# A vision tower on one core: third bf16 part on GpSimd, the rows of the maxima sent a step sooner, twelve more unread products, five projections moved forward

## The chip, the core and the metric

The kernel runs on one core of a Trainium2 chip. The core has TensorE (PE, matrix products into PSUM), VectorE (DVE), ScalarE (ACT), GpSimd (POOL) and SyncE (SP, which here only issues transfers); they run on their own and wait for each other by semaphores. The metric is the device time of one execution in microseconds. An execution is timed several times, and one more is run with the hardware profiler.

## The reference

The input holds four sequences of 512 tokens of 256 channels. Four blocks follow, each but the first with a residual sum and a layer norm:

```python
h = relu(x @ W0.T) * (x @ W1.T) @ Wo.T                  # gated unit, DE = 512
h = layernorm(h + window_attention(h))                  # 16 heads of 16, |i - j| <= 64
h = layernorm(h + quantised_ffn(h))                     # 8-bit activations, ternary weights, 1024 wide
h = layernorm(h + causal_attention(h))                  # 16 heads of 16
scores = softmax(h @ wg); gates, idx = top_k(scores, 2) # 8 experts, capacity 640 rows each
y = combine(gates, expert(dispatch(h, idx)))            # silu(x @ fc1.T + b1) @ fc2 + b2
out = layernorm(h + y) * gamma + beta
```

Softmax, norms and the expert layers are in float32. The scores of the attention must keep float32 accuracy.

## The kernel before, in words

**Two halves.** Up to about 603 us the kernel computes everything before the experts, then the eight experts one after the other (until about 898 us), then the last norm. The change touches the first part and the seam between the two.

**Half steps.** The first part is a pipeline that is written out by hand. A unit `u` is one tile of 128 keys for four heads of one batch; there are 128 units, 64 of the window attention and 64 of the causal one. Every unit takes two half steps, `eta`, and each engine runs through the same list `HALVES` of half steps and does in each what is due: TensorE the scores of half step `eta` and the transposed scores, values and back transposes of units that began 15, 19 and 28 half steps earlier (`TO_TURNED`, `TO_VALUES`, `TO_BACK`). A batch has 32 half steps, numbered 32 i to 32 i + 31 for the eight pairs (layer, batch) i. In the profile a half step takes some 2 us.

**Dense work.** The table `DENSE` (L98) says at which half step the other phases of each batch begin: `tok` the gated unit, `qkv` the projections, `o` the output projection and its norm, `ffn` the quantised layer, `gate`, `route` and `send` the routing. `STEPS` says how many steps a phase has, and `stretched` (L154) puts the steps of a `qkv` phase from batch 2 on two half steps apart. In each half step an engine does its attention work and then `dense` for each phase in the order of the table. The eight PSUM banks are dealt out by `take` (L179) from the same table, so the banks follow a change of it.

**Projections in three parts.** A float32 projection is kept as three bf16 parts whose products add up to float32 accuracy. Step c of `qkv` has TensorE make piece j = c − 1 (queries and keys of eight heads, two blocks: four pieces), ScalarE copy it twice from PSUM, as float32 into `proj` (L766, two buffers) and as bf16 into `parts` (L767). One step later VectorE takes the difference in place (L1340) and GpSimd rounds it to the second part (L598). One step later still VectorE takes the rest as the third part (L1335). SyncE copies the parts into the stacks `qs` and `ks` (L499), a ring of three blocks of heads, twelve transfers of 128 KB a block; it waits for the ring place, and ScalarE waits with the next batch's piece for the copies of the last (`stack_in`) and for the third part two pieces back (`part2_done`).

**Rows of the maxima.** The transposed scores need the negated row maxima as three more rows of `qs`. VectorE finds the maxima (L1156), GpSimd splits them into three parts (`split_maxima`, L577 to L583), TensorE turns them (L874), ScalarE copies them out (`rows`, L659) in half step 8 g + 11 and issues the transfer into `qs` (`send_rows`, L666) at the start of half step 8 g + 12, after all that it does in step 8 g + 11. TensorE reads them with the transposed scores of step 8 g + 15 (L889).

**Port to the experts.** After the last row transfer of the routing (L619) the rows of expert 0 are loaded and turned (L1547), and the first layer (L1562) follows. To keep TensorE from standing still, 26 products whose result nobody reads (L1582) run before, released by GpSimd seven transfers into the last `send`.

## Time and profile before

| | |
|---|---|
| median of 3 runs | 938.91 us (934.48 to 941.21) |
| profiled execution | 940.09 us, span 938.2 us |
| PE busy | 838.0 us, 89% |
| DVE busy | 513.8 us, 55% |
| ACT busy | 434.0 us, 46% |
| POOL busy | 342.1 us, 36% |
| mean granted clock | 0.947 |
| L1335, third part | 32, 23.4 us of DVE |
| L1340, difference | 32, 24.4 us of DVE |
| L598, second part | 32, 20.8 us of POOL |
| L1582, unread products | 26, 7.3 us of PE |

The span is that of the instructions; the rest of an execution's time lies around it. Busy time is counted per engine over the whole span, so a share of it says nothing of a stretch in which another engine is the one waited for. The granted clock is that of TensorE, 1.0 being 2.4 GHz and 0.5 being 1.2 GHz.

### The profile page before, as it was taken

The page shows a single profiled execution, that of the slowest core. Times are in us where ns is not written, and L with a number is a line of the kernel's source. Part 1 is how long each engine was busy: PE and PEld are TensorE (multiplying, and loading weights), DVE is VectorE, ACT ScalarE, POOL GpSimd, SP SyncE. Part 2 cuts the span into 40 slices and gives each one's busy share as a digit, 9 for nine tenths or more (in the row PEclk, how much of TensorE's full clock was granted, in tenths as well). Part 3 has the DMA queues.
Part 4 walks back from the last instruction along what each step waited for, and adds up shares of the span by engine and source line. Part 5 has one row for each costly group of instructions (what it writes and reads, how often), then busy time and mean ns, then how long its engine had stood idle before and what let it go on. Part 6 is the DMA issues. An engine that isn't in the chain of part 4 may idle for free.

```text
span 938.2 us, 14078 instructions
## 1 busy us (share of the span) xinstructions
PE 838.0 (89%) x4784; PEld 537.0 (57%) x4784; DVE 513.8 (55%) x1929; ACT 434.0 (46%) x794; POOL 342.1 (36%) x517
## 2 busy tenths in 40 slices
PE   6999999898898899899999897499999999999920
PEld 2565546555555455355454354267787787887820
DVE  5676335779798798688887763230220221221246
ACT  1525335687787887887566563122112112112006
POOL 6124224635445343233463634620220320321422
PEclk9999999999999899999898997789999999999965
DMA  9662021212211220210333106311514514512342
GB/s 341 210 233 72 24 69 51 61 29 69 70 34 38 69 65 11 64 52 19 114 92 92 48 24 241 109 51 45 152 18 135 151 17 135 147 22 61 35 111 90
DMA packets 58663, 81.48 MB, mean 87 GB/s; under 512 B 8160, under 2 KB 52193, under 8 KB 56160
## 3 DMA queue, kind: packets, MB, share of 16 engines
q1 hardware_dynamic: 49520, 70.48, 23.4%
q0 software_dynamic: 7296, 9.47, 6.0%
q10 hardware_dynamic: 1776, 0.63, 0.3%
q8 instruction: 38, 0.62, 0.3%
q14 instruction: 33, 0.27, 0.1%
HBM read 35.37 MB, written 19.68 MB: 59 GB/s over the span
## 4 chain that ended last, share of the span: by engine, by line
PE 69%; DVE 15%; issue 5%; ACT 5%; POOL 3%; DMA 2%; SPq 0%; ACTq 0%; POOLq 0%; DVEq 0%
PE ps L1562 15%; PE ps L1576 15%; PE ps L956 6%; PE ps L905 5%; PE ps L1002 4%; DVE junk L1156 4%; PE ps L867 4%; PE ps L889 4%; PE ps L1028 3%; PE ps L973 3%; PE ps L922 2%; PE ps L1011 2%; ACT probs L681 1%; DVE sm L1306 1%; PE ps L932 1%
## 5 line engine op out<-in xcount | busy, mean ns | idle before, releaser
L1156 DVE CUSTOM_DVE_ANT_0 junk<-ps,maskb 128x256 bf16<-128x256 f32 (+4 forms) x512 | 200.3, 435 | 74.1 <-PE ps L867 73.8
L681 ACT ACTIVATE probs<-ps 128x512 f32<-128x512 f32 (+1 forms) x304 | 157.3, 552 | 66.9 <-PE ps L889 64.8
L1600 ACT ACTIVATE hTe<-ps,qs 128x640 f32<-128x640 f32 x64 | 50.8, 794 | 221.1 <-PE ps L1562 221.1
L1517 POOL DMA_INDIRECT mixed_rows<-ysb,ids x40 | 62.0, 1551 | 223.9 <-DVE ysb L1675 220.9
L1576 PE MATMUL ps<-ks,hTe 128*128 128x256 f32 x640 | 143.3, 379 | 0.0
L1562 PE MATMUL ps<-dxT,qs 128*128 128x320 f32 x512 | 142.8, 439 | 0.5 <-DVE dxT L1653 0.5
L1576 PEld LDWEIGHTS ps<-ks,hTe 128*128 128x128 f32 x640 | 119.3, 190 | 15.1
L1562 PEld LDWEIGHTS ps<-dxT,qs 128*128 128x128 f32 x512 | 98.5, 193 | 41.0 <-issue 2.0
L889 PE MATMUL ps<-qs,ks 99*128 99x256 bf16 (+4 forms) x512 | 104.0, 289 | 10.8 <-DMA qs<-nrows 5.6
L867 PE MATMUL ps<-ks,qs 96*128 96x256 bf16 (+4 forms) x512 | 106.0, 290 | 2.9 <-DVE nmax L1156 1.4
L905 PE MATMUL ps<-probs,vaug 128*32 128x256 f32 (+4 forms) x1024 | 89.9, 425 | 7.5 <-POOL probs L557 3.8
L867 PEld LDWEIGHTS ps<-ks,qs 96*128 96x128 bf16 x512 | 44.3, 100 | 81.2 <-issue 64.0
L1653 DVE COPY dxT<-ps 128x256 f32<-128x256 f32 x40 | 16.8, 420 | 130.4 <-PE ps L1547 130.4
L562 POOL TENSOR_SCALAR_AFFINE_SELECT probs<-probs 128x256 f32<-128x256 f32 (+1 forms) x64 | 41.0, 641 | 109.6 <-ACT probs L681 109.6
L1672 DVE TENSOR_TENSOR ysb<-ps,ks 128x256 f32<-128x256 f32 x40 | 17.0, 425 | 110.2 <-PE ps L1576 110.2
L956 PE MATMUL ps<-x_sb,tokw 128*128 128x512 f32 x128 | 62.6, 624 | 7.5 <-DMA tokw<-w 7.5
L557 POOL TENSOR_SCALAR_AFFINE_SELECT probs<-probs 128x512 f32<-128x512 f32 x64 | 41.0, 642 | 73.1 <-ACT probs L681 72.9
L889 PEld LDWEIGHTS ps<-qs,ks 99*128 99x128 bf16 x512 | 43.8, 100 | 37.2 <-DVE nmax L1156 7.8
L1002 PE MATMUL ps<-actT,aw 128*128 128x512 f32 x128 | 60.5, 598 | 1.9 <-issue 1.1
L905 PEld LDWEIGHTS ps<-probs,vaug 128*32 128x32 f32 x1024 | 20.8, 110 | 38.7 <-issue 24.3
L1156 DVE DVE_READ_ACCUMULATOR2_ANT nmax<- 128x1 f32 x512 | 42.3, 83 | 0.0
L956 PEld LDWEIGHTS ps<-x_sb,tokw 128*128 128x128 f32 x128 | 23.6, 198 | 31.8 <-issue 31.6
(198 smaller groups left out, 1223.8 us busy)
## 6 DMA issues: line engine op xcount, KB each, us to landing
qs<-parts SPq DMA_DIRECT2D x96, 128.0 KB, 2.4
ks<-parts SPq DMA_DIRECT2D x96, 128.0 KB, 2.4
qs<-w SPq DMA_DIRECT2D x8, 1024.0 KB, 9.4
ks<-w SPq DMA_DIRECT2D x8, 1024.0 KB, 4.9
dispatched_rows<-att SPq DMA_DIRECT2D x8, 650.0 KB, 10.6
ks<-dispatched_rows SPq DMA_DIRECT2D x4, 650.0 KB, 7.3
x_sb<-xT SPq DMA_DIRECT2D x8, 256.0 KB, 3.8
mixed_rows<-h SPq DMA_DIRECT2D x4, 512.0 KB, 3.1
```

Source lines behind the costliest of these rows:

```text
L557: pool.affine_select(out=p[:, :, 0:P], in_=p[:, :, 0:P], compare_op=ALU.is_ge, fill=0.0, base=0, pattern=[[0, HG], [1, P]], channel_multip ...
L681: act.activation(probs_of(u)[:, heads[0]:heads[-1] + 1, :], turned_bank((u, half, i))[:, 0:len(heads) * w].rearrange("p (j n) -> p j n", n=w),
L867: ins = mm(o[:, a * (hi - lo):(a + 1) * (hi - lo)], qs[0:KS, r, hd, t * P:(t + 1) * P], ks[0:KS, r, hd, lo:hi], start=True, stop=True)
L889: ins = mm(o[:, a * (hi - lo):(a + 1) * (hi - lo)], ks[0:KM, r, hd, kt * P:(kt + 1) * P], qs[0:KM, r, hd, lo:hi], start=True, stop=True)
L905: ins = mm(bank(V_BANK)[32 * j:32 * j + 32, lo:hi], vaug[:, s % NV, kt, hd * SLOT:hd * SLOT + 32], p[:, j, :], start=(kt == 0), stop=(kt = ...
L956: ins = mm(o, tokw[:, k, col:col + P], x_sb[:, k, :], start=(k == 0), stop=(k == KD - 1))
L1002: ins = mm(o, w[:, k, col:col + P], actT[:, k, :], start=(k == 0), stop=(k == KD - 1))
L1156: ins = dve.tensor_tensor_reduce(out=junk[:, b - (b > V_BANK), a * (hi - lo):(a + 1) * (hi - lo)], in0=score_bank((u, half, i))[:, a * (hi ...
L1517: pool.indirect_dma_start(out=acc, out_offset=bass.IndirectOffsetOnAxis(ap=ids[:, e, t:t + 1], axis=0), in_=ysb[:, e % 2, t, :], in_offset ...
L1562: ins = mm(bank(2 * (n % 2) + c)[:, 0:HC], w1s[:, e % 2, k, m * P:(m + 1) * P], dxT[:, e % 2, k, c * HC:(c + 1) * HC], start=(k == 0), sto ...
L1576: ins = mm(bank(4 + n % 2)[:, 0:D], hTe[:, e % 2, m, t * P:(t + 1) * P], w2s[:, e % 2, m, :], start=(m == 0), stop=(m == MH - 1))
L1600: act.activation(hTe[:, e % 2, m, :].rearrange("p (a n) -> p a n", a=2), ps[:, 2 * (n % 2):2 * (n % 2) + 2, 0:HC], ACT.Silu, bias=b1s[:, e ...
```

## The change

Four things are changed.

- The third part is taken by GpSimd, right behind its rounding of the second part, and no longer by VectorE a step later. It waits for its own rounding.
- ScalarE issues the transfer of the rows in the half step in which it copied them, after the exponentials of that half step and before its dense work.
- The unread products are 38 and not 26.
- The projections of batches 3, 4, 5 and 6 begin four half steps sooner, those of batch 7 eight.

VectorE also waits for its own copy of the mask, in half step −4.

```diff
-WARM_AT, WARM = 7, 26
+WARM_AT, WARM = 7, 38
...
-    ("qkv", 3, 66), ("o", 1, 86), ("ffn", 1, 93), ("qkv", 4, 98), ("o", 2, 118), ("ffn", 2, 125), ("qkv", 5, 130),
-    ("o", 3, 150), ("ffn", 3, 157), ("qkv", 6, 162), ("o", 4, 182), ("gate", 0, 186), ("route", 0, 188),
-    ("send", 0, 196), ("qkv", 7, 196), ("o", 5, 213), ("gate", 1, 217), ("route", 1, 219), ("send", 1, 228),
+    ("qkv", 3, 62), ("o", 1, 86), ("ffn", 1, 93), ("qkv", 4, 94), ("o", 2, 118), ("ffn", 2, 125), ("qkv", 5, 126),
+    ("o", 3, 150), ("ffn", 3, 157), ("qkv", 6, 158), ("o", 4, 182), ("gate", 0, 186), ("route", 0, 188),
+    ("send", 0, 196), ("qkv", 7, 188), ("o", 5, 213), ("gate", 1, 217), ("route", 1, 219), ("send", 1, 228),
...
                         pool.wait_ge(rest_done, n + 1)
                         pool.tensor_copy(parts[:, c - 2, 1, :], proj[:, c % 2, :]).then_inc(part1_done, 1)
+                        pool.wait_ge(part1_done, n + 1)
+                        pool.tensor_tensor(parts[:, c - 2, 2, :], proj[:, c % 2, :], parts[:, c - 2, 1, :],
+                                           ALU.subtract).then_inc(part2_done, 1)
...
-                    if e % 8 == 1 and 0 <= e < 2 * UNITS + 1:
-                        send_rows(e // 8)
                     for step in SCHED.get(eta, ()):
                         early(*step)
                     e = eta - TO_TURNED
                     if 0 <= e < 2 * UNITS:
                         exps(*divmod(e, 2))
+                    e = eta - TO_ROWS
+                    if e % 8 == 0 and 0 <= e < 2 * UNITS:
+                        send_rows(e // 8)
                     for step in SCHED.get(eta, ()):
                         dense(*step)
...
-                        j = c - 3
-                        if 0 <= j < 2 * NB:
-                            dve.wait_ge(part1_done, 2 * NB * i + j + 1)
-                            dve.tensor_tensor(parts[:, j, 2, :], proj[:, j % 2, :], parts[:, j, 1, :],
-                                              ALU.subtract).then_inc(part2_done, 1)
...
                         dve.tensor_copy(maskb[:, :], mask_in).then_inc(mask_done, 1)
+                        dve.wait_ge(mask_done, 1)
```

How the order of instructions moves is shown at three places, all around the feed-forward layer of batch 0 (`ffn` 0, half steps 61 to 89) or the end of the norm of the next batch. The same instruction stands at another line in the changed kernel (L666 at L669, L718 at L721, L1306 at L1310, L1340 at L1339).

ScalarE in half steps 91 and 92, at the norm of batch 1: `nrows` are the rows, `probs` exponentials, `h` the four normalisations. Before:

```order
L681 ACTIVATE probs<-ps 128x512 [waits filled0]
L659 ACTIVATE nrows<-ps 48x128 [waits nmax_in0,filled7]
L681 ACTIVATE probs<-ps 128x512 [waits filled1,pv_mm]
L718 ACTIVATE h<-att,mv,rstd 128x256 [waits shift_done]
L718 ACTIVATE h<-att,mv,rstd 128x256
L666 DMA qs<-nrows 3x16x128 [waits read7]
L681 ACTIVATE probs<-ps 128x512 [waits filled2]
L718 ACTIVATE h<-att,mv,rstd 128x256 [waits shift_done]
L718 ACTIVATE h<-att,mv,rstd 128x256
```

In the changed kernel:

```order
L684 ACTIVATE probs<-ps 128x512 [waits filled2]
L662 ACTIVATE nrows<-ps 48x128 [waits nmax_in0,filled7]
L684 ACTIVATE probs<-ps 128x512 [waits filled0,pv_mm]
L669 DMA qs<-nrows 3x16x128 [waits read7]
L721 ACTIVATE h<-att,mv,rstd 128x256 [waits shift_done]
L721 ACTIVATE h<-att,mv,rstd 128x256
L684 ACTIVATE probs<-ps 128x512 [waits filled1]
L721 ACTIVATE h<-att,mv,rstd 128x256 [waits shift_done]
L721 ACTIVATE h<-att,mv,rstd 128x256
```

The transfer L666 stood behind the two normalisations that wait for `shift_done`; it now stands ahead of them, behind one exponential.

VectorE in the heavier of the half steps of a feed-forward tile (half step 74): `sm` are scales of the quantisation, `proj` and `parts` those of the projections. Before:

```order
L1299 TENSOR_TENSOR work<-work,ps 128x512
L1306 TENSOR_REDUCE sm<-work 128x1
L1309 TENSOR_SCALAR sm<-sm 128x1
L1312 RECIPROCAL sm<-sm 128x1
L1314 TENSOR_SCALAR sm<-sm 128x1
L1316 TENSOR_SCALAR sm<-sm,wsc 128x1
L1335 TENSOR_TENSOR parts<-proj,parts 128x512
L1340 TENSOR_TENSOR proj<-proj,parts 128x512
```

In the changed kernel, the same half step and the first score maximum of the next:

```order
L1303 TENSOR_TENSOR work<-work,ps 128x512
L1310 TENSOR_REDUCE sm<-work 128x1
L1313 TENSOR_SCALAR sm<-sm 128x1
L1316 RECIPROCAL sm<-sm 128x1
L1318 TENSOR_SCALAR sm<-sm 128x1
L1320 TENSOR_SCALAR sm<-sm,wsc 128x1
L1160 ISA junk,nmax<-ps,maskb 128x256
```

The third part and the difference behind it are gone from this half step; the difference stands in steps 66, 68, 70 and 72 instead of 70, 72, 74 and 76.

GpSimd around the projections of batch 3: `probs` are the selects of the window, `parts` the rounding. Before:

```order
L562 AFFINE_SELECT probs<-probs 128x4x64 [waits read1]
L565 AFFINE_SELECT probs<-probs 128x4x128
L598 CAST parts<-proj 128x512 [waits rest_done]
L562 AFFINE_SELECT probs<-probs 128x4x128 [waits read3]
L565 AFFINE_SELECT probs<-probs 128x4x128
L598 CAST parts<-proj 128x512 [waits rest_done]
L562 AFFINE_SELECT probs<-probs 128x4x128 [waits read0]
L565 AFFINE_SELECT probs<-probs 128x4x128
L598 CAST parts<-proj 128x512 [waits rest_done]
```

In the changed kernel:

```order
L562 AFFINE_SELECT probs<-probs 128x4x128 [waits read4]
L565 AFFINE_SELECT probs<-probs 128x4x128
L598 CAST parts<-proj 128x512 [waits rest_done]
L600 TENSOR_TENSOR parts<-proj,parts 128x512 [waits part1_done]
L562 AFFINE_SELECT probs<-probs 128x4x128 [waits read4]
L565 AFFINE_SELECT probs<-probs 128x4x128
L598 CAST parts<-proj 128x512 [waits rest_done]
L600 TENSOR_TENSOR parts<-proj,parts 128x512 [waits part1_done]
L562 AFFINE_SELECT probs<-probs 128x4x128 [waits read2]
L565 AFFINE_SELECT probs<-probs 128x4x64
```

Behind each rounding stands the third part, and the next two selects come after it.

## Rows read from the trace of the kernel before

**Rows 1.** The page, the chain that ended last, by engine

```profile
PE 69%; DVE 15%; issue 5%; ACT 5%; POOL 3%; DMA 2%; SPq 0%; ACTq 0%; POOLq 0%; DVEq 0%
```

**Rows 2.** Busy time by stretch: length, PE, PEld, DVE, ACT, POOL, granted clock, DMA

```profile
170.80:190.80 20.00, 17.61 (x146) 11.53 (x144) 15.62 (x75) 14.25 (x30) 10.10 (x24) 0.91 0.30 81
190.80:233.40 42.60, 39.12 (x304) 23.25 (x303) 37.00 (x132) 35.03 (x61) 21.59 (x40) 1.00 0.14 39
...
295.80:316.90 21.10, 18.84 (x144) 12.07 (x143) 16.83 (x80) 15.60 (x32) 10.31 (x21) 0.84 0.28 77
316.90:364.70 47.80, 43.92 (x303) 23.01 (x303) 42.30 (x135) 37.71 (x65) 18.93 (x36) 1.00 0.13 35
...
466.00:486.00 20.00, 20.00 (x129) 10.14 (x127) 15.55 (x57) 14.44 (x30) 14.50 (x23) 1.00 0.38 113
```

**Rows 3.** Chain of waits, first heavy stretch: start, length, what

```profile
200.49 0.61 DVE parts L1335
...
211.99 1.04 DVE proj L1340
...
216.20 1.23 DVE sm L1306
```

**Rows 4.** Timeline of ScalarE and TensorE: start, length, what, idle before and releaser

```profile
176.48 0.26 ACT L659 ACTIVATE nrows<-ps 48x128 bf16<-48x128 bf16 x1
...
179.66 0.76 ACTq L666 DMA_DIRECT2D qs<-nrows  x1
...
182.12 0.34 PE L889 MATMUL ps<-qs,ks 99*128 99x192 bf16 x2 [1.59 <-DMA qs<-nrows]
```

**Rows 5.** Who waited for whom: total, times, longest

```profile
PE ps L889 <- DMA qs<-nrows: 5.6, 4, 1.6
```

**Rows 6.** TensorE by stretch: length, PE busy, granted clock, DMA share, GB/s

```profile
184.00:187.00 3.00, 3.00 (x20) 0.50 0.55 148
...
307.00:313.50 6.50, 6.50 (x43) 0.51 0.74 201
...
382.50:385.00 2.50, 2.50 (x19) 0.50 0.15 43
...
600.20:603.90 3.70, 3.70 (x19) 1.00 0.28 102
```

**Rows 7.** Instructions grouped by line and shape

```profile
L1335 DVE TENSOR_TENSOR parts<-proj,parts 128x512 bf16<-128x512 f32 x32 | 23.4, 732 | 1.6 <-POOL parts L598 1.5
...
L766 ACT ACTIVATE proj<-ps,ab 128x512 f32<-128x512 f32 x32 | 22.0, 687 | 33.2 <-PE ps L1002 24.8 <-DVE parts L1335 4.6 <-issue 3.7
...
L767 ACT ACTIVATE parts<-ps,ab 128x512 bf16<-128x512 f32 x32 | 21.8, 680 | 0.0
```

**Rows 8.** Chain of waits, products of one projection piece and of expert layers

```profile
190.95 1.72 PE ps L1002 x4
...
611.25 9.60 PE ps L1562 x24
...
668.32 17.23 PE ps L1562 x64
```

**Rows 9.** One line, GpSimd's bias sum: ns shortest, median, longest

```profile
L606 POOL TENSOR_TENSOR h<-h,ar x16: 1264/1272/2241, 62.2 to 487.8; 128x512 f32<-128x512 f32 x16
```

**Rows 10.** Timeline of TensorE at the unread products and behind them

```profile
596.86 7.33 PE L1582 MATMUL ps<-qgu,identb 128*128 128x512 bf16 x26 [5.65 <-POOLq L612]
607.51 1.14 PE L1547 MATMUL ps<-cst,qs 128*128 128x128 f32 x4 [3.33 <-DMA qs<-dispatched_rows]
```

**Rows 11.** Timeline of SyncE's queue, and landing of its stack copies (shortest, median, longest)

```profile
185.53 3.79 SPq L499 DMA_DIRECT2D ks<-parts  x6
...
DMA to landing us min/median/max: 2.3/2.4/4.0
```

**Rows 12.** Timeline of GpSimd and VectorE side by side

```profile
82.82 1.27 POOL L606 TENSOR_TENSOR h<-h,ar 128x512 f32<-128x512 f32 x1
82.89 1.75 DVE L1335 TENSOR_TENSOR parts<-proj,parts 128x512 bf16<-128x512 f32 x1 [0.16 <-POOL parts L598]
```

## The prediction, made before the changed kernel was run

> **What bounds the kernel now.** I read the page first: the chain that ended last is TensorE for 69% and VectorE for 15% [rows 1]. The second view is the table of busy time by stretch, cut at the products of the output projections, which come once per batch: a light stretch (attention alone, while normalisation and quantisation run through) and a heavy one (feed-forward tiles and the next projections). For the first batch these are 20.0 and 42.6 us, for the third 21.1 and 47.8 us [rows 2]. There are four such pairs, between 170.8 and 436.9 us. TensorE is busy 39.12 of 42.60 us in a heavy stretch, but VectorE 37.00 and ScalarE 35.03, so all three pass work on and any can be the one waited for. The chain of waits says which: through 200 to 219 us it runs over VectorE, and over three lines in it that this change touches or relieves, the third part (0.61 and 0.70 us), the subtraction behind it (1.04) and the row maximum of a tile (1.23) [rows 3]. In the light stretches the end is set by TensorE and one wait. From 436.9 us on TensorE is full (20.00 of 20.00 us in one window [rows 2]); from 611 us to the last expert it is TensorE without gaps.
>
> The sum is made against the profiled execution, 940.09 us for a span of 938.2; the median of the runs is 1.2 us below it.
>
> **Rows of the maxima.** ScalarE copies them at 176.48 us and issues their transfer only at 179.66: between the two stand two of the four normalisations, which wait for GpSimd, as the transfer belongs to the next half step. TensorE stands still for 1.59 us until 182.12 [rows 4]. There are four such waits, 5.6 us together [rows 5]. The order of ScalarE shows the transfer now ahead of the first normalisation, some 3 us earlier, so the rows land before they are read. Behind the issue stands only that normalisation, which waits for GpSimd anyway. I take all of it: −5.6 us; the ends are −2.8 (half is refilled by VectorE being late at the next bank) and −5.6.
>
> Behind each of these waits the granted clock falls to its lower level, 1.2 GHz: 3.0 us at 184 us (the second batch has one like it), 6.5 us at 307, 2.5 us at 382.5, each with TensorE busy throughout [rows 6]. That is 15.0 us at half speed, worth 7.5 us. If the wait goes, the engine is denser there. But the heavy stretches get thinner by what is moved out of them, and a fall can come there. Ends 0 and −7.5; I take the middle, −3.75 us.
>
> **Third part and projections sooner.** A batch has four projection pieces. A third part costs VectorE 0.732 us [rows 7]. In the order all four leave VectorE's heavy stretch, and with the projections two half steps apart and four sooner one subtraction leaves it too (0.70), and the three that stay meet no third part, so the 0.34 us that 1.04 stands above its neighbour goes [rows 3]: 4 × 0.732 + 0.70 + 0.34 = 3.97 us less on VectorE. ScalarE loses two pieces of 0.687 + 0.680 us, 2.73 [rows 7], TensorE two of 1.72 us, 3.44 [rows 8]. A stretch that all three share shortens by about the smallest of these to the largest: 2.73 to 3.97 us; I take 3.0, near the smallest since ScalarE is nearly as busy: four times, −12.0 us. The light stretch takes the same 3.44 us of products. TensorE is idle there for 20.00 − 17.61 = 2.4 us [rows 2], of which 1.6 is the wait already counted, so 0.8 us is filled: +2.6 each, +10.6 us (ends +2.6 and +3.44 each). Nearly a wash; it pays by what it takes from VectorE, not by moving.
>
> The third part on GpSimd is two inputs of 128x512; the nearest row is GpSimd's bias sum of the same size, 1.272 us [rows 9]. Four of them bring GpSimd in a heavy stretch to at most 21.59 + 4 × 1.27 = 26.7 of 42.6 us [rows 2]. It has slack, and its next select is two half steps off. SyncE sends the third part, and ScalarE overwrites its source, in the same steps as before; the part is now made in the half step of the cast and not in the next one, so it is not late for either. Covered, at nothing; uncovered it would be the last rival.
>
> The Trainium skill, GPSIMD Engine Reference, section Engine selection, gives elementwise work to VectorE since GpSimd is about twice as slow with two inputs; 1.272 over 0.732 is 1.7, so the trace agrees. By that rule alone the sum would be 32 × 0.54 = 17 us of engine time worse; it says nothing of which engine is waited for.
>
> Projections 0, 1 and 2 stay, under a full TensorE: nothing. The wait of VectorE on its own mask copy (half step −4) is one short wait behind a copy, before the first score: nothing. Projection 7 goes eight half steps sooner inside a full TensorE: nothing, but GpSimd has there 14.50 of 20 us filled already, with eight row transfers [rows 2]; four third parts add 5.1 us, all now beside the transfers. Selects may be late. Ends 0 and +3; I take +1.0 us.
>
> **The unread products.** The 26 end at 604.19 us (596.86 + 7.33); the first rows arrive at 607.51 [rows 10]. After that pause the granted clock is at 1.2 GHz and stays there up to about 617 us: 24 products of the first layer of expert 0 take 9.60 us, where 64 take 17.23 at the upper level [rows 8], that is 6.46 for 24: 3.1 us lost. Twelve more at some 0.22 us (19 in 3.70 us [rows 6]) end at 606.8, before the rows, so they delay nothing, and the pause shrinks from 3.3 to 0.7 us. −3.1 us; ends 0 (the clock falls all the same, as the rows come one by one and TensorE is half idle up to 611.25) and −3.6 (the transposes too).
>
> **Sum:** −5.6 − 3.75 − 12.0 + 10.6 − 3.1 + 1.0 = −12.9 us: 927.2 for a profiled execution, **926** against the median. The best ends give −5.6 − 7.5 − 15.9 + 10.6 − 3.6 = −22, 917; the worst −2.8 − 0 − 10.9 + 13.8 − 0 + 3 = +3.1, 942.
>
> **Rivals.**
> *The gaps fill again (25%).* VectorE is busy 37 of 42.6 us and 15.6 of 20; with the row wait gone it may be late at the next bank, and the clock falls as before. For it: 0.8 us of TensorE's light idle has other causes already. Then −2.8 + 0 − 12.0 + 10.6 − 3.1 + 1.0 = −6.3: 933.
> *The clock falls before expert 0 all the same (10%).* Only the last term goes: 929.
> *Projections meet the stack (8%).* ScalarE may write the third piece of a batch only when the twelve copies of the batch before have landed. SyncE starts them when the ring is free, the last issue ends at 185.53 + 3.79 = 189.3, and landing takes 2.4 us: 191.7 [rows 11]. The third piece is now due near 190.8 − 3.3 + 2.6 + 1.7 = 191.8. If the half steps between get faster by 2 us, ScalarE waits 2 us, four times: 934.
> *GpSimd holds VectorE (7%), the slower one.* The trace has GpSimd and VectorE in each other's way: a sum of GpSimd from 82.82 us, and the third part of VectorE beside it took 1.75 us instead of 0.73 [rows 12]. A third part on GpSimd is such a sum. If every one of them catches a subtraction or a quantisation of VectorE, each costs up to 1.27 us: 4 × 1.27 = 5.1 per heavy stretch against the 3.97 saved, +1.1 each; with the moved products in the light stretches, the clock as before and the rest as forecast, −5.6 + 4.4 + 10.6 − 3.1 + 1.0 = +7.3: 946. It decides from three in four on. Against it: in the order two to four score maxima follow each subtraction on VectorE, 0.3 to 0.4 us each with one operand in PSUM, and cast and sum run beside them. The Trainium skill, SBUF — State Buffer, section "SBUF: two separate sides", calls the pair of ports an exclusive lock that a GpSimd instruction or a VectorE one with two SBUF inputs holds to its end; the 1.75 us agrees. By that rule alone each overlap blocks in full, which is the price used here.
>
> **Chances.** The forecast, 922 to 931, has 50%. A measurement of this kernel tells about 1% from no change: 929.5 and 948.3. Faster by more takes nearly all of the forecast, half of the 929 case and a little of the first rival: 0.55. Within 1%: 0.40. Slower: 0.05, of the last rival. The range that holds the time 8 times in 10 is 918 to 938: both sides of the first and third rival are in, the last rival and the outermost ends out.
>
> **What would show it.** Right: no wait of the transposed scores on the row transfer; no stretch of the lower clock just behind half step 61 of batches 0 to 3; heavy stretches 3 us shorter than before (39.6 for the first, 44.8 for the third) and light ones no longer than before; VectorE's total down by 23 us, GpSimd's up by 41; the first 24 products of expert 0 in 6.5 us. Wrong: light stretches longer than before by more than 1 us; VectorE's subtractions or quantisations at 1.3 us or more beside a third part on GpSimd; ScalarE's projection copies waiting for stacked parts; expert 0 still at the lower clock; TensorE waiting on selects in 460 to 500 us.

## The result

| | before | after |
|---|---|---|
| median of 22 runs each | 936.96 us (934.48 to 941.21) | 933.87 us (931.58 to 937.62) |
| ratio | | 0.9963, interval 0.9951 to 0.9975 |
| profiled execution, span | 940.09, 938.2 us | 933.26, 931.5 us |
| DVE, POOL busy | 513.8, 342.1 us | 499.0, 377.7 us |
| mean granted clock | 0.947 | 0.955 |

The change saves 3.1 us by the medians (3.5 by the ratio), where 12.9 were forecast; 926 was said. The 933.87 lies outside the 922 to 931 of the forecast itself and inside the 918 to 938 that was to hold 8 times in 10. A caution for the reading: the profiled execution of before lies 3.1 us above its own median, so the 6.8 us between the two profiles are about half a difference between executions.

### The profile page after: what moved, and what is told of

The parts are those of the page before. It is cut to its first block, busy times and chain, and to the rows that moved or that the text cites. A ratio compares the mean times of both kernels' runs of the same rounds, so it can differ in the third digit from the quotient of the medians.

```text
span 931.5 us, 14103 instructions
## 1 busy us (share of the span) xinstructions
PE 832.8 (89%) x4796; PEld 535.5 (57%) x4796; DVE 499.0 (54%) x1897; ACT 432.7 (46%) x794; POOL 377.7 (41%) x549
## 4 chain that ended last, share of the span: by engine, by line
PE 72%; DVE 10%; ACT 6%; issue 6%; POOL 5%; DMA 1%; SPq 0%; POOLq 0%; ACTq 0%; DVEq 0%
PE ps L1576 15%; PE ps L1562 15%; PE ps L960 6%; PE ps L1006 5%; PE ps L909 5%; PE ps L871 4%; PE ps L893 4%; PE ps L1032 3%; PE ps L977 3%; DVE junk L1160 2%; PE ps L1015 2%; ACT probs L684 2%; PE ps L926 2%; POOL dispatched_rows L622 2%; PE ps L1042 1%
## 5 line engine op out<-in xcount | busy, mean ns | idle before, releaser
L1562 PE MATMUL ps<-dxT,qs 128*128 128x320 f32 x512 | 139.9, 433 | 0.5 <-DVE dxT L1653 0.5
```

Of the source, the lines that this page charges most:

```text
L1562: ins = mm(bank(2 * (n % 2) + c)[:, 0:HC], w1s[:, e % 2, k, m * P:(m + 1) * P], dxT[:, e % 2, k, c * HC:(c + 1) * HC], start=(k == 0), sto ...
```

## The profile after

The page, busy time by engine and the chain that ended last:

```profile
PE 832.8 (89%) x4796; PEld 535.5 (57%) x4796; DVE 499.0 (54%) x1897; ACT 432.7 (46%) x794; POOL 377.7 (41%) x549
...
PE 72%; DVE 10%; ACT 6%; issue 6%; POOL 5%; DMA 1%; SPq 0%; POOLq 0%; ACTq 0%; DVEq 0%
```

VectorE's share of the chain fell from 15% to 10%, GpSimd's rose from 3% to 5% [rows 1].

Busy time by stretch, cut at the same half steps as [rows 2] (light, heavy, light, heavy):

```profile
171.00:192.70 21.70, 19.82 (x154) 12.07 (x152) 16.31 (x75) 16.15 (x34) 11.80 (x26) 1.00 0.28 75
192.70:233.40 40.70, 37.94 (x296) 23.39 (x295) 34.78 (x129) 32.83 (x57) 24.17 (x42) 0.92 0.15 41
295.20:316.80 21.60, 19.70 (x152) 11.85 (x151) 17.45 (x80) 17.16 (x36) 11.64 (x23) 1.00 0.28 75
316.80:360.90 44.10, 40.09 (x296) 21.57 (x295) 39.12 (x131) 35.38 (x61) 22.13 (x38) 1.00 0.14 38
```

The heavy stretches are 1.9 and 3.7 us shorter (3.0 were forecast), the light ones 1.7 and 0.5 us longer. The clock is at 1.00 in the light stretches and no longer 0.91 and 0.84, but the first heavy one has 0.92 where before had 1.00: the low clock went from the light stretch into the thinned heavy one.

Instructions grouped by line and shape, total and mean in ns:

```profile
L600 POOL TENSOR_TENSOR parts<-proj,parts 128x512 bf16<-128x512 f32 x32 | 38.8, 1212 | 2.7
L1339 DVE TENSOR_TENSOR proj<-proj,parts 128x512 f32<-128x512 f32 x32 | 25.9, 809 | 9.1 <-ACT parts L770 9.1
```

The third part takes 1.21 us on GpSimd against 0.73 on VectorE [rows 7]. VectorE's total fell by 14.8 and not by 23.4 us. The subtraction rose from 24.4 to 25.9 and the scaling of `work` (L1322, now L1326) from 11.7 to 13.7. The largest single piece has nothing to do with the third part: a cast of the row numbers that took 0.41 us in the kernel before stands for 4.05 us beside GpSimd's sums of the expert biases (3.47 us in s_warm, where the third part is still VectorE's):

```profile
606.55 4.05 DVE L1634 CAST ids<-qs 128x5 uint32<-128x5 f32 x1
```
```profile
605.76 4.82 POOL L1509 TENSOR_TENSOR aw<-h,qs 128x256 f32<-128x256 f32 x7
```

TensorE at the unread products and behind them:

```profile
592.86 11.07 PE L1582 MATMUL ps<-qgu,identb 128*128 128x512 bf16 x38 [5.97 <-POOLq L615]
603.76 0.60 PE L1547 MATMUL ps<-cst,qs 128*128 128x128 f32 x4
...
606.69 6.73 PE L1562 MATMUL ps<-dxT,qs 128*128 128x320 f32 x24 [0.52 <-DVE dxT L1653]
```

The first 24 products of expert 0 take 6.73 us instead of 9.60 [rows 8]. There is no idle time ahead of the transposes: the products end when the first rows have landed or later.

The wait of TensorE on the row transfer [rows 5] is gone from the list of waits. The timeline around half step 60 says why that gains nothing. ScalarE, with its queue of transfers, and then GpSimd:

```profile
176.71 0.26 ACT L662 ACTIVATE nrows<-ps 48x128 bf16<-48x128 bf16 x1
176.99 0.60 ACT L684 ACTIVATE probs<-ps 128x512 f32<-128x512 f32 x1
177.01 0.76 ACTq L669 DMA_DIRECT2D qs<-nrows  x1
179.88 1.09 ACT L721 ACTIVATE h<-att,mv,rstd 128x256 f32<-128x256 f32 x2 [2.29 <-POOL mv L592]
180.88 0.57 ACT L684 ACTIVATE probs<-ps 128x512 f32<-128x512 f32 x1
```
```profile
178.52 1.04 POOL L588 TENSOR_TENSOR rstd<-mv,neg_half 128x4 f32<-128x4 f32 x1 [0.41 <-DVE mv L1195]
179.64 0.20 POOL L592 TENSOR_TENSOR mv<-mv,rstd 128x4 f32<-128x4 f32 x1
181.52 0.64 POOL L562 TENSOR_SCALAR_AFFINE_SELECT probs<-probs 128x512 f32<-128x512 f32 x1 [1.68 <-ACT probs L684]
```

The transfer leaves at 177.01, right behind the copy. But ScalarE waits 2.29 us for the norm's root on GpSimd, all the same; the exponentials stand behind it at 180.88, the selects at 181.52. The chain of waits of the kernel before had this path already:

```profile
178.29 1.05 POOL rstd L588
...
179.65 0.60 ACT h L718
...
180.65 0.58 ACT probs L681
...
181.29 0.64 POOL probs L562
181.93 0.60 POOL probs L565
...
182.57 0.64 PE ps L905 x8
```

It ends at 182.57, 0.45 us behind the end of the wait on the transfer [rows 4]. Whatever the transfer did, the next values could not start sooner. Half steps 60 to 64 take 6.09 us in the kernel before and 6.09 in the changed one.

## The experiments

All are medians against the kernel before on the same chip, 6 to 12 runs each and 22 for the whole change. The kernels were measured on several chips, so they are compared with each other by the ratio. Intervals are some 0.2% (2 us) to each side, for some kernels of six runs 0.3%, so one difference of 2 us proves little, and comparisons that repeat count for more.

The executions of one kernel differ, in part with the granted clock. Those of p_third_warm fall into seven of 928.6 to 929.8 us, with a mean clock of 0.953 or 0.954, and three of 933.9 to 934.6, with 0.948 to 0.950. Its profile is of one of the three. So a difference between two profiles counts for much only where several profiles show it.

| kernel | median | ratio (interval) |
|---|---|---|
| s_rows: rows sooner | 939.85 | 1.0026 (1.0008 to 1.0044) |
| s_third: third part | 931.75 | 0.9937 (0.9912 to 0.9961) |
| s_warm: 38 products | 934.57 | 0.9966 (0.9945 to 0.9987) |
| s_proj: projections 3 to 7 | 944.73 | 1.0063 (1.0038 to 1.0088) |
| s_proj36: projections 3 to 6 | 940.68 | 1.0034 (1.0013 to 1.0056) |
| s_proj7: projections 7 | 939.28 | 1.0020 (0.9999 to 1.0040) |
| p_third_warm | 929.62 | 0.9925 (0.9902 to 0.9948) |
| p_third_warm_rows | 932.71 | 0.9947 (0.9927 to 0.9968) |
| p_third_warm_proj36 | 930.66 | 0.9927 (0.9903 to 0.9950) |
| p_third_warm_proj | 933.99 | 0.9963 (0.9942 to 0.9985) |
| p_all_but_proj7 | 931.34 | 0.9921 (0.9892 to 0.9951) |
| the whole change | 933.87 | 0.9963 (0.9951 to 0.9975) |
| p_fill: whole, 6 more products a tile | 940.15 | 1.0015 (0.9994 to 1.0036) |
| t_qkv7_192 | 933.46 | 0.9938 (0.9916 to 0.9959) |
| t_qkv7_200 | 929.96 | 0.9909 (0.9880 to 0.9937) |
| t_warm32 | 929.30 | 0.9908 (0.9889 to 0.9927) |
| t_warm50 | 932.29 | 0.9947 (0.9924 to 0.9970) |
| v_best | 928.13 | 0.9900 (0.9868 to 0.9932) |
| v_best_proj36 | 928.47 | 0.9910 (0.9880 to 0.9939) |

### Each part alone

**s_rows**, the transfer of the rows alone.

```diff
-                    if e % 8 == 1 and 0 <= e < 2 * UNITS + 1:
-                        send_rows(e // 8)
...
+                    e = eta - TO_ROWS
+                    if e % 8 == 0 and 0 <= e < 2 * UNITS:
+                        send_rows(e // 8)
```

> The kernel before with one edit: the transfer of the rows is issued in the half step in which they were copied. Theory (the row transfer shared its wait with the values, which wait for the same normalisations through ScalarE's exponentials and GpSimd's select): time within 1 us of before, the 1.6 us waits of L889 on the transfer gone, and waits of the values (L905) on the select or a later start of the half steps 60 to 64 in their place. Rival (the prediction's: the transfer alone held TensorE): 5 to 9 us faster, half steps 60 to 64 of each batch 1.6 us shorter.

Measured 0.26% slower. In its list of waits one on the transfer is left of the four:

```profile
PE ps L906 <- POOL probs L565: 2.6, 3, 0.9
...
PE ps L890 <- ACT probs L681: 2.4, 3, 0.8
...
PEld ps L890 <- DMA qs<-nrows: 0.6, 1, 0.6
```

The first two have no entry in the kernel before: waits on the selects and on the exponentials took the place of those on the transfer. Half steps 60 to 64 take 6.08 us, as before (6.09). So 5.6 us of wait went and no time with it, which is the theory, though its "within 1 us of before" is missed by the 0.26% (2.4 us). The rival's 5 to 9 us did not come. Added to the other parts, the same edit moved the ratio by +0.0022 (beside third part and products), −0.0006 (with projections 3 to 6 as well) and 0.0000 (with all of them). It gains nothing; whether it costs 2 us in a kernel that is otherwise as before is not shown beyond the one comparison.

**s_third**, the third part on GpSimd alone.

```diff
+                        pool.wait_ge(part1_done, n + 1)
+                        pool.tensor_tensor(parts[:, c - 2, 2, :], proj[:, c % 2, :], parts[:, c - 2, 1, :],
+                                           ALU.subtract).then_inc(part2_done, 1)
```

> The kernel before with the third part taken by GpSimd behind the second (and VectorE's wait on its mask copy). Theory (VectorE is on the chain in the heavy stretches, and cast and sum run under the score maxima): 2 to 4 us faster, by about a third part per heavy stretch. Rival (GpSimd's sums hold VectorE at the shared port): 0 to 5 us slower, with differences L1340 or quantisations L1322 of 1.1 us and more beside a third part. Rival 2 (VectorE is not what the heavy stretch waits for): within 1 us.

0.63% faster, 5.9 us: more than the 2 to 4 of the theory, and both rivals fall. By ratio it is more than the whole change, though the ends of the two intervals overlap. The stretches, cut at the half steps of [rows 2] (heavy of the first and of the third batch):

```profile
190.90:231.20 40.30, 38.49 (x301) 23.35 (x303) 34.93 (x128) 34.78 (x61) 25.84 (x44) 1.00 0.15 41
312.70:358.50 45.80, 42.89 (x300) 23.08 (x302) 39.67 (x130) 37.29 (x66) 23.32 (x40) 1.00 0.13 37
```

40.3 and 45.8 us against 42.6 and 47.8, with the projections where they were. The whole change, with the projections moved out as well, has 40.7 and 44.1: in the first of the two this edit alone gives all of the gain, in the third it gives 2.0 of 3.7. What the projections add over all four is in the table of stretches below.

**s_warm**, 38 products alone.

```diff
-WARM_AT, WARM = 7, 26
+WARM_AT, WARM = 7, 38
```

> The kernel before with 38 unread products. Theory (the clock stays at its upper level through the row loads): 2.5 to 3.3 us faster, the first 24 products of expert 0 in 6.5 to 6.8 us instead of 9.6. Rival (it falls all the same in part of the executions, as TensorE is half idle while the rows come): 0 to 1.5 us faster on the median.

0.34% faster, 3.2 us: as forecast.

**s_proj**, the projections moved alone (the table's lines as in the change).

> The kernel before with the projections of batches 3 to 6 four half steps sooner and of batch 7 eight. Theory (what the heavy stretches gain is lost to a lower clock in their thinned tail in the first two batches, and batch 7 loses 3 to 5 us beside the row transfers): within 2 us of before, on either side. Rival (the prediction's: a small gain from heavy stretches 3 us shorter): 1 to 6 us faster.

0.63% slower. Both theories of this expectation fall: this part is a loss, not a wash.

### The ladder

**p_third_warm**, s_third and s_warm together.

> The kernel before with two parts of the change: the third bf16 part on GpSimd and 38 unread products; rows and projections as before. Theory A (what the four parts do alone adds up when they lie in different stretches, and these two do: the third part in the stretches 130 to 590 us, the products at 593 to 604 us): the gains alone were 0.63% and 0.34% of 937 us, so 5.9 + 3.2 = 9.1 us less, 928 us, ratio 0.990. Theory B (the gain of the products was a difference between executions, since the one profile of that kernel is only 3 us shorter in its whole span): 931 to 932 us, ratio 0.994. By A this is faster than the whole change (0.9963) by 6 us, and the other two parts of the change cost that.

0.9925; 7.0 us of the 9.1. Between the theories, and 3.6 us faster than the whole change by ratio.

**p_third_warm_rows**, with the rows sooner.

> The kernel before with three parts of the change: third part, products and rows of the maxima sent in their half step; the projections of batches 3 to 7 stay where they were. Theory A (sending the rows sooner shortens nothing, because the next half step's normalisations end late by the path of the values through GpSimd and ScalarE, and alone it measured 2.5 us more): 928 to 931 us, within 2 us or some 2 us above the kernel without it. Theory B (the rows sent sooner cost only because VectorE was full; with the third part gone from VectorE they give the 3 to 5 us forecast): 923 to 925 us. Against the whole change this leaves the projections alone: if they cost 7.6 us as alone, this kernel is 5 to 8 us faster than the whole change; if they cost nothing beside the relieved VectorE, both are at 934 us.

0.9947. Not the 3 to 5 us that a relieved VectorE should have let through: theory A.

**p_all_but_proj7**, the whole change with batch 7 as before.

```diff
-    ("send", 0, 196), ("qkv", 7, 188), ...
+    ("send", 0, 196), ("qkv", 7, 196), ...
```

> The whole change, but with the projections of batch 7 at half step 196 again; those of batches 3 to 6 stay four half steps sooner. Theory A (the loss of the moved projections lies with batch 7: between half steps 188 and 204 the kernel after gives back 5.1 us against before, where routing, sends and projections meet, TensorE is thin and its clock low): about 5 us less than the whole change, 929 us, ratio 0.991. Theory B (it lies with batches 3 to 6, whose projections fill stretches in which VectorE is the bound): within 1 us of the whole change, 934 us, ratio 0.996.

0.9921 against 0.9963: batch 7's eight half steps cost 3.9 us, between the theories and nearer to A.

**p_fill**, against the low clock in the thinned heavy stretches.

```diff
+                            if t in (2, 3):
+                                for _ in range(6):
+                                    mm(o, identb[:, :], qgu[:, 0, 0:S], start=True, stop=True)
                             pe.wait_ge(*d_out(("ffn", i, f"f{t}")))
```

> The whole change, and before the waits of the second product of the feed-forward layer (its third and fourth tile of 512 columns) six unread bf16 products each, into the bank that is then overwritten. Theory A (the low clock in the tails of the heavy stretches, at 223, 284 and 441 us, comes from TensorE having stood still so often in the stretch before, and costs about 1 us each): the products stand mostly in TensorE's waits, the clock stays high, 1 to 4 us less, 930 to 933 us. Theory B (these products delay the scores and normalisations behind them more than the clock gives): 12 products of 0.22 to 0.24 us for each of six batches are 16 to 17 us of TensorE, of which a third to a half lands on the path, 939 to 943 us.

Two stretches of the whole change, and the same of this kernel (the tail of the first heavy stretch, and the whole third one):

```profile
223.00:230.00 7.00, 6.27 (x38) 4.27 (x39) 5.67 (x25) 3.77 (x7) 2.43 (x4) 0.52 0.03 7
314.80:360.20 45.40, 41.39 (x306) 22.47 (x303) 40.23 (x132) 36.91 (x63) 23.37 (x38) 1.00 0.14 37
```
```profile
223.00:230.00 7.00, 6.90 (x70) 4.44 (x70) 6.51 (x29) 5.99 (x11) 3.89 (x6) 1.00 0.04 11
314.40:362.20 47.80, 44.10 (x319) 23.68 (x316) 40.63 (x132) 37.12 (x63) 23.63 (x40) 1.00 0.13 35
```

The products lift the clock of the tail from 0.52 to 1.00, as wanted, and the kernel is 5 us slower than the whole change. There are 48 such products (four batches have the layer, and not six as the expectation has it), 11.7 us of TensorE by the profile. They cost more than the clock gave; theory B, at the lower figure. The profiles say where. The first two heavy stretches, whose clock was low, are 0.6 and 0.3 us shorter with them; the third and fourth, whose clock was at 1.00 without them, are 2.4 and 2.3 us longer. The same products in the first two batches alone were not tried.

### The projections

**s_proj36** and **s_proj7**, the two halves of that move alone.

> The kernel before with the projections of batches 3 to 6 alone four half steps sooner; those of batch 7 as before, and no other part of the change. The projections of all five batches alone cost 7.6 us. Theory A (most of that is batch 7, whose projections lie eight half steps sooner beside routing and sends; in that kernel's trace half steps 188 to 200 take 24.2 us against 19.9 before): 938 to 940 us, ratio 1.001 to 1.003. Theory B (half or more lies with batches 3 to 6, because the third part on VectorE fills the stretches that these projections enter): 941 to 943 us, ratio 1.004 to 1.006.

> The kernel before with the projections of batch 7 alone at half step 188 instead of 196. Theory A (batch 7 is the loss): 941 to 943 us, ratio 1.004 to 1.006. Theory B (half or more of the loss is with batches 3 to 6): 938 to 940 us. The two single moves should add up to the 7.6 us of both; if they add to less, the rest is an effect of one on the other.

+3.2 and +1.9 us, together 5.1 of the 5.9 that both cost by ratio. The first lies between its theories; the second is theory B, at least half of the loss with batches 3 to 6.

**p_third_warm_proj36** and **p_third_warm_proj**, the same beside third part and products.

> Third part on GpSimd, 38 products, projections of batches 3 to 6 four half steps sooner; rows and batch 7 as before. Theory A (from the ladder so far: rows cost 2.1 to 2.7 us, these projections bring 2.4 us once VectorE has no third part): 2.4 us below the kernel with third part and products alone, 927 us, ratio 0.990, and the best of all. Theory B (the ladder's steps of 2 us are within its intervals, and neither rows nor these projections do anything): 929 to 931 us, ratio 0.992 to 0.993.

> The whole change without the rows of the maxima, which are sent as before. Theory A (rows cost 2 us wherever they are added): 932 us, ratio 0.994. Theory B (rows do nothing here; the loss against third part and products alone is the projections'): within 1 us of the whole change, 934 us, ratio 0.996. Against the kernel of this call with the projections of batches 3 to 6 alone it gives the price of batch 7 once more: 4 us in the ladder so far.

0.9927 and 0.9963 beside 0.9925 without, theory B of both: once the third part is off VectorE, batches 3 to 6 cost nothing (+0.2 us) and bring nothing, and batch 7 costs 3.4 us. This is the interaction that the singles hide: their four ratios add up to 0.9992 (1 + 0.0026 − 0.0063 − 0.0034 + 0.0063), and the whole is 0.9963.

The profiles show the same interaction. The four light stretches together (half steps 56 to 68, 88 to 100, 120 to 132, 152 to 164), the four heavy ones (68 to 88 and so on to 184), and both, in us, each from the start of the first score product of a half step:

| kernels | light | heavy | both |
|---|---|---|---|
| third part on VectorE (before, s_warm, s_proj7; means) | 78.0 | 187.6 | 265.5 to 265.7 |
| the same, rows sooner (s_rows) | 77.2 | 189.0 | 266.3 |
| the same, projections 3 to 6 moved (s_proj36, s_proj) | 82.8 | 184.9 | 267.7 |
| third part on GpSimd (seven kernels; means) | 77.5 | 181.4 | 257.2 to 259.9 |
| the same, rows sooner (p_third_warm_rows) | 80.3 | 179.7 | 260.0 |
| the same, projections 3 to 6 moved (three kernels) | 82.8 | 175.2 | 258.0 |
| whole change; p_all_but_proj7 | 82.8 | 176.7; 175.5 | 259.5; 258.4 |

The projections of batches 3 to 6 make the light stretches some 5 us longer in either kernel. With the third part on VectorE they take only 2.7 us off the heavy ones, a loss; with it on GpSimd they take 6.2 off, and the two ends cancel. Rows sooner gains nothing in any pair.

The same code also has two lengths, by the granted clock. The first heavy stretch (half steps 68 to 88) of s_third and of p_third_warm, which are alike there:

```profile
189.10:230.80 41.70, 39.84 (x311) 24.32 (x312) 36.04 (x133) 36.30 (x63) 26.13 (x44) 1.00 0.16 43
```
```profile
189.80:232.60 42.80, 41.27 (x314) 25.29 (x311) 36.23 (x133) 36.39 (x63) 25.83 (x44) 0.96 0.16 42
```

The lower level inside the second one costs 1.1 us.

For batch 7, half steps 188 to 200 and 200 to 232 (where the first score product of the half step starts), in p_third_warm and then in p_third_warm_proj:

```profile
441.10:463.20 22.10, 19.48 (x125) 8.19 (x125) 17.69 (x76) 11.47 (x24) 8.29 (x16) 0.85 0.37 109
463.20:518.80 55.60, 53.23 (x361) 26.93 (x357) 40.59 (x175) 34.55 (x72) 32.05 (x52) 0.94 0.30 85
```
```profile
439.00:462.70 23.70, 22.74 (x144) 11.02 (x144) 21.06 (x80) 15.19 (x32) 13.20 (x20) 1.00 0.34 96
462.70:517.70 55.00, 49.31 (x342) 24.05 (x338) 37.24 (x171) 30.29 (x64) 27.08 (x48) 0.88 0.31 88
```

The stretch that receives the projections grows by 1.6 us, while its clock rises from 0.85 to 1.00. The stretch that they leave is only 0.6 shorter. What left it are twelve products of 512 columns and eight of 256 (L1005 and L1014), 7.7 us of TensorE. TensorE's busy time there fell by 3.9 us only, since the granted clock went from 0.94 to 0.88 and products that stayed took longer. And it is idle for 5.7 us instead of 2.4, so the length hardly changed. In p_third_warm:

```profile
L1005 PE MATMUL ps<-actT,aw 128*128 128x512 f32 x12 | 5.7, 601 | 0.0
...
L908 PE MATMUL ps<-probs,vaug 128*32 128x512 f32 x32 | 5.1, 719 | 0.0
...
L1014 PE MATMUL ps<-aw,actT 128*128 128x256 f32 x16 | 3.9, 386 | 0.9 <-ACT parts L770 0.9
```

and in p_third_warm_proj, without L1005:

```profile
L908 PE MATMUL ps<-probs,vaug 128*32 128x512 f32 x32 | 6.8, 938 | 0.0
...
L1014 PE MATMUL ps<-aw,actT 128*128 128x256 f32 x8 | 1.9, 378 | 0.0
```

The two executions are not alike: the first lies 4.3 us above its kernel's median, the second 1.6 below. But all profiles agree. In the five with the projections at 188, half steps 188 to 200 take 23.7 to 24.4 us (mean 24.1) and 200 to 232 have a clock of 0.85 to 0.93 (mean 54.0 us). In the eleven with 196, the first take 19.6 to 22.6 us (21.2), and the others have 0.94 to 1.00 (54.7 us). The move costs 2.9 us at one end and gives back 0.6 at the other.

**t_qkv7_192** and **t_qkv7_200**, the same projections at two other places in p_third_warm.

> Third part on GpSimd and 38 products, with the projections of batch 7 at half step 192 (196 in the kernel that measured 929.6 us, 188 in the whole change). Theory A (the loss of batch 7 comes from meeting the routing of half steps 188 to 194 on VectorE): half of the meeting is gone, 930 to 932 us, ratio 0.993 to 0.995, and half steps 188 to 200 take 21 to 23 us instead of 24. Theory B (the loss comes from anything sooner than the sends, since the sends then stand in half steps without projections that could cover them): as the whole move, 933 to 934 us, ratio 0.996.

> The same kernel with the projections of batch 7 at half step 200, four later than before. Theory A (the routing is what the projections should stay away from; half steps 196 to 207 have sends on GpSimd): equal to 196 within 1 us, 929 to 931 us, ratio 0.992 to 0.993. Theory B (each half step later brings something, because the sends alone fill GpSimd at 196 to 203 and the third parts stand behind them): 926 to 928 us, ratio 0.988 to 0.990. Theory C (too late: the scores of batch 7 wait for its stacks): 932 to 936 us.

At 188, 192, 196 and 200 the ratios are 0.9963, 0.9938, 0.9925, 0.9909. Half steps 188 to 200 take 23.7, 22.5, 22.1 and 19.4 us in these four traces, half steps 200 to 232 take 55.0, 56.3, 55.6 and 57.7. The order goes one way and each step is within the intervals; the ends, 0.0054 apart, are not. That 188 is worse than 200 is shown; that later is better step by step, also past the routing, is not. The traces do not settle it: with the projections at 196 half steps 188 to 200 take 19.6 to 22.6 us from one profile to another. Place 192 fits theory A by its ratio and its 22.5 us, and theory B by its median; 200 is between A and B.

### The products

**t_warm32** and **t_warm50**, p_third_warm with other numbers of products.

> Third part on GpSimd with 32 unread products instead of 38. Theory A (the clock is up when the experts begin if the products end just before; with 38 they end about when the first rows land, so that six fewer leave a gap of 1.4 us in which nothing is lost, and the clock stays): 929 to 930 us as with 38. Theory B (the gap of 1.4 us or the shorter run of products lets the clock be low for the first experts, as with 26): 932 us, the 24 products of L1561 near 9.6 us instead of 6.7.

> Third part on GpSimd with 50 unread products instead of 38. Theory A (with 38 the products already end when the first rows have landed, 603.76 us and no idle time before the transposes): each further product stands in the way at 0.22 us at full clock, 12 x 0.22 = 2.6 us more, 932 us, ratio 0.995. Theory B (the low clock before the experts, 14 us from 586 us on, ends sooner or the last wait hides them): 929 to 930 us.

TensorE with 32 (31 of them recorded) and with 50 products:

```profile
588.86 9.19 PE L1581 MATMUL ps<-qgu,identb 128*128 128x512 bf16 x31 [6.37 <-POOLq L615]
598.72 0.86 PE L1546 MATMUL ps<-cst,qs 128*128 128x128 f32 x4 [0.67 <-DMA qs<-dispatched_rows]
...
602.23 6.73 PE L1561 MATMUL ps<-dxT,qs 128*128 128x320 f32 x24 [0.51 <-DVE dxT L1652]
```
```profile
594.90 13.48 PE L1581 MATMUL ps<-qgu,identb 128*128 128x512 bf16 x49 [6.38 <-POOLq L615]
...
611.15 1.08 PE L1561 MATMUL ps<-dxT,qs 128*128 128x320 f32 x3 [0.52 <-DVE dxT L1652]
```

With 32 the pause is 0.67 us, expert 0 still runs at 6.73, and from the start of the products to that of expert 0 it is 13.37 us; with 38 it is 13.83 (592.86 to 606.69), and 14.07 in p_third_warm. So the last products of the 38 stand in the way, by 0.5 to 0.7 us. With 50 it is 16.25 us, 2.2 to 2.4 more (2.1 by ratio). Theory A of both.

### A better kernel

**v_best**: third part, 32 products, batch 7's projections at 200, nothing else. **v_best_proj36**: batches 3 to 6 moved as well.

```diff
-WARM_AT, WARM = 7, 26
+WARM_AT, WARM = 7, 32
...
-    ("send", 0, 196), ("qkv", 7, 196), ...
+    ("send", 0, 196), ("qkv", 7, 200), ...
```

> The kernel before with the third part on GpSimd, 32 unread products, and the projections of batch 7 at half step 200; rows and batches 3 to 6 as before. Theory A (the steps add up: 0.9925 with 38 products and 196; 0.9908 with 32; 0.9909 with 200): 0.989, 927.5 us. Theory B (both steps of 0.0016 are within their intervals and nothing is gained): 0.9925, 930 us.

> The same with the projections of batches 3 to 6 four half steps sooner. Theory A (they bring nothing: 0.9927 against 0.9925 beside the third part and 38 products): equal to the other kernel of this call within 1.5 us. Theory B (they bring 1 to 2 us, as in the profiles of half steps 60 to 156, which are 1 to 1.5 us shorter with them): 926 us, ratio 0.9875.

0.9900 and 0.9910. The first is 1.0% faster than before and 0.6% faster than the whole change, with intervals that do not touch; moving batches 3 to 6 brings nothing here either, theory A. The steps add up to within their uncertainty (0.989 expected by theory A of v_best).

## Why the forecast was 9.8 us off

The 9.8 us are two things. The sum was made for a profiled execution, 940.09 us; the profile of the changed kernel is 6.8 us below it, so the sum was 6.1 us off. The other 3.7 are executions: the profile of before lies 3.1 us above its median of 22 runs, that of the changed kernel 0.6 below its own. Of the 6.1 us, 4.5 lie in the four pairs of stretches: rows, clock, heavy and light were summed to −10.75 there, and the two profiles differ by −6.2 (265.7 and 259.5).

- **Rows of the maxima, −5.6: wrong, and the largest miss; measured 0 (or a loss).** The step said that ScalarE's normalisation behind the issue "waits for GpSimd anyway" and drew from it that the issue is free. It is. But the same wait holds the exponentials and selects that TensorE's next values need, and it ends 0.45 us behind the wait on the transfer. A wait in the list was booked as time without asking what ends next; the chain of waits printed just that. This is the step that failed.
- **Low clock behind the waits, −3.75: mostly moved, not removed.** The clock rose to 1.00 in the light stretches, and fell in the first two heavy ones (both 0.92 between half steps 68 and 88, and 100 and 120). p_fill, which keeps it up there, pays more for that than it gets. The price was too high as well: for the code that ran at a mean clock of 1.00 and of 0.96 the sum's rule gives 0.04 × 42.8 = 1.7 us, and the difference was 1.1.
- **Heavy stretches, −12.0: nearly right.** The four measured 187.3 and 176.7, −10.6. By the table of stretches about half of that comes from the third part and half from the projections, so both sources of the step were real.
- **Light stretches, +10.6: mis-sized, measured +4.4** (78.4 and 82.8). Milder than forecast, so this makes up part of the 9.35 us that rows and clock were to bring and did not; that the sum came no further off is luck. Heavy and light together were −1.4; the runs give −5.9 for the third part and, beside it, +0.2 for batches 3 to 6. Here the forecast asked too little.
- **GpSimd and batch 7, +1.0; measured +3.4 and +3.9.** The step argued that a move "inside a full TensorE" costs nothing. The full window that it read, 466 to 486 us, is the stretch that the projections leave; the one that they enter, half steps 188 to 200, had TensorE busy for 18.83 of 19.90 us only and at a mean clock of 0.84:

```profile
446.90:466.80 19.90, 18.83 (x124) 8.55 (x125) 17.48 (x76) 10.78 (x24) 9.11 (x16) 0.84 0.43 128
```

  And the full one gives back little of what is taken from it, since its clock falls and its waits grow. Of the 3.4 us the pair of profiles shows 1.0; over all profiles with 188 and with 196, half steps 188 to 232 average 78.2 and 75.9 us, 2.3. Where the rest lies is not placed.
- **Unread products, −3.1: right**, −3.2 alone, with the pause gone and the 24 products at 6.73 instead of the 6.46 worked out.
- **GpSimd as bound and in VectorE's way, the slower rival: not borne out in size.** Side by side a subtraction did take 1.12 us where the median is 0.69:

```profile
192.00 1.12 DVE L1339 TENSOR_TENSOR proj<-proj,parts 128x512 f32<-128x512 f32 x1
```
```profile
191.42 1.16 POOL L600 TENSOR_TENSOR parts<-proj,parts 128x512 bf16<-128x512 f32 x1
```

  GpSimd's ends at 192.58; the subtraction that was issued at 192.00 ends 0.54 us after that, less than the 0.69 it takes in all, so it stood still for most of the overlap. The Trainium skill (SBUF — State Buffer, section "SBUF: two separate sides") describes an exclusive lock, under which the second instruction waits for the whole of the first. The trace agrees to within 0.15 us. Over all 32 subtractions it is 1.5 us more (24.4 to 25.9), and perhaps the 2.0 of the 16 scalings, against 23.4 us taken off.
- **The stack rival** did not come: ScalarE's projection copies wait once for 0.2 us on a stacked part. "The gaps fill again" named the right time, 933, with VectorE as the cause; it was GpSimd and ScalarE of the norm. That its figure fits is in part luck, as its sum was −6.3 and the medians differ by 3.1.
- **The signs.** Of those for "right", the wait on the transfer, the clock behind half step 61 and the 24 products came; VectorE's −23 us (−14.8) and GpSimd's +41 (+35.6) did not. Of those for "wrong", one came: the first two light stretches are more than 1 us longer.

The sum of what was measured part by part beside the others: third part and products −7.0, batch 7 +3.4, the rest 0: −3.6 for a change that measured −3.5 by ratio. As p_third_warm_proj and the whole change measured the same ratio, this says that the parts are consistent, and proves none of them anew.

## What to carry to other kernels

A wait in the list is worth only what the next wait behind it leaves: before booking it, follow the other operands of the instruction behind it to their own end in the chain. Work that is moved between two stretches has a price at each end, and neither is the length of the work: 7.7 us of TensorE gave back 0.6 and cost 2.9. Read both stretches, the one that it enters above all, and test each move apart and beside the others, for what was a loss in the kernel before (batches 3 to 6) was a wash once VectorE was relieved. A slower engine can be the right place for work if the faster one is waited for: 1.21 us on GpSimd instead of 0.73 on VectorE, 32 times, gained 5.9 us.

## What the runs showed of the hardware

- A thinner TensorE was granted less: with 7.7 us of products taken from a stretch of 55 us its clock fell from 0.94 to 0.88. Twelve unread products a batch lifted a stretch of 7 us from 0.52 to 1.00 and cost more time over the kernel than they gave.
- The same instructions ran in 41.7 us at a mean granted clock of 1.00 (s_third, t_warm32, v_best) and in 42.8 at 0.96 (p_third_warm, t_qkv7_200). The executions of p_third_warm at a mean clock of 0.953 or 0.954 took 928.6 to 929.8 us, those at 0.948 to 0.950 took 933.9 to 934.6.
- A VectorE cast of 128x5, 0.16 us elsewhere, stood for 4.05 us beside GpSimd's bias sums, which ran without a pause from 605.76 to 610.58 us.
- After a pause of 0.67 us ahead of the transposes the next products still ran at the upper level (6.73 us for 24); after one of 3.33 us they did not (9.60 us).
